# First pair of a two-stage token kernel: GpSimd's own order, b2 as a split row on TensorE, low parts last in group 0

## What is computed

```
h   = relu(x @ W1[lang] + b1[lang])                 # 512 -> 128
y   = x + h @ W2[lang] + b2[lang]                   # 128 -> 512
x1  = x + (y - mean(y)) * rsqrt(var(y) + 1e-5) * gamma[lang] + beta[lang]
g   = gelu(x1 @ M1 + c1)                            # 512 -> 2048
out = x1 + concat(g @ M2 + c2, g @ E[expert] + e[expert])   # 384 and 128 columns
```

## Time and profile before

| | |
|---|---|
| median of 3 runs | 1502.94 us |
| profiled execution | 1501.87 us |
| its span | 1499.8 us |
| TensorE matmul busy | 1460.2 us, 97% |
| VectorE, ScalarE, GpSimd busy | 941.4, 519.4, 648.9 us |
| granted TensorE clock, mean | 0.99 |

### The profile page before, as it was taken

One profiled execution on the slowest core, in us unless ns is written; L12 is line 12 of the kernel. 1 busy time (PEld: TensorE's weight loads), 2 busy tenths in 40 slices (PEclk: granted clock), 3 DMA queues, 4 the chain that ended last, 5 costly groups with the idle time before them and its releaser, 6 DMA issues.

```text
span 1499.8 us, 19043 instructions
## 1 busy us (share of the span) xinstructions
PE 1460.2 (97%) x6428; PEld 1191.3 (79%) x6428; DVE 941.4 (63%) x1598; ACT 519.4 (35%) x837; POOL 648.9 (43%) x641
## 2 busy tenths in 40 slices
PE   8779899999999999999999999999999999999999
PEld 4567788778888888888888888888888888888887
DVE  4757776667557675567655766657755767554444
ACT  1633334323253333432353322532325333332321
POOL 5492534635148341473335533463514834153111
PEclk9989999999999999999999999999999999999999
DMA  7636546655355644645556453665535663454332
GB/s 259 224 108 222 195 155 238 218 165 190 132 179 209 200 153 144 239 163 176 176 170 237 164 171 130 228 218 165 190 126 177 216 200 124 150 173 163 119 139 89
DMA packets 127760, 265.90 MB, mean 177 GB/s; under 512 B 11696, under 2 KB 83632, under 8 KB 119472
## 3 DMA queue, kind: packets, MB, share of 16 engines
q1 hardware_dynamic: 117296, 157.73, 33.0%
q10 hardware_dynamic: 10368, 106.96, 18.9%
HBM read 226.90 MB, written 37.75 MB: 176 GB/s over the span
## 4 chain that ended last, share of the span: by engine, by line
PE 81%; POOL 7%; DMA 3%; DVE 3%; issue 2%; ACT 1%; SPq 1%; POOLq 0%; DVEq 0%; ACTq 0%
PE down L220 14%; PE down L222 14%; PE down L221 14%; PE up_b L220 5%; PE up_b L221 5%; PE up_b L222 5%; PE up_c L220 3%; PE up_a L222 3%; PE up_a L221 3%; PE up_a L220 3%; PE up_c L221 3%; PE up_c L222 3%; POOL resid L855 3%; DMA w_raw<-m_we 2%; DMA w_raw<-m_w 1%
## 5 line engine op out<-in xcount | busy, mean ns | idle before, releaser
L220 PE MATMUL down<-w,g 128*128 128x512 f32 x1024 | 402.8, 393 | 3.4 <-issue 2.8
L221 PE MATMUL down<-w,g 128*128 128x512 f32 x1024 | 399.9, 391 | 0.0
L222 PE MATMUL down<-w,g 128*128 128x512 f32 x1024 | 399.9, 390 | 0.0
L862 POOL TENSOR_TENSOR w<-w_raw,ones 128x256 fp32r<-128x256 f32 x128 | 90.4, 706 | 628.8 <-DMA w_raw<-m_we 628.8
L621 DVE TENSOR_TENSOR g<-g_raw,g 128x512 fp32r<-128x512 f32 x256 | 203.5, 807 | 225.4 <-ACT g L468 225.4
L220 PEld LDWEIGHTS down<-w,g 128*128 128x128 f32 x1024 | 193.4, 189 | 44.8 <-issue 3.2
L222 PEld LDWEIGHTS down<-w,g 128*128 128x128 f32 x1024 | 193.2, 189 | 40.7
L221 PEld LDWEIGHTS down<-w,g 128*128 128x128 f32 x1024 | 193.4, 189 | 39.5
L466 ACT ACTIVATE g_raw<-up_a,m_b_sb 128x512 f32<-128x512 f32 x64 | 44.2, 690 | 372.0 <-PE up_a L222 371.9
L468 ACT CAST g<-g_raw 128x512 fp32r<-128x512 f32 x256 | 159.1, 621 | 8.1
L220 PE MATMUL up_b<-bo,w 128*128 128x512 f32 x384 | 149.7, 390 | 1.4 <-DVE bo L707 1.2
(11 more groups left out here) (165 smaller groups left out, 2360.7 us busy)
## 6 DMA issues: line engine op xcount, KB each, us to landing
w<-w_kept ACTq DMA_DIRECT2D x56, 1792.0 KB, 7.9
w<-w_kept SPq DMA_DIRECT2D x56, 768.0 KB, 5.3
w_raw<-m_we SPq DMA_DIRECT2D x128, 128.0 KB, 4.8
out<-resid SPq DMA_DIRECT2D x64, 256.0 KB, 4.8
xTs_raw<-xT SPq DMA_DIRECT2D x56, 256.0 KB, 3.0
w_kept<-w SPq DMA_DIRECT2D x8, 1792.0 KB, 7.5
xs<-x SPq DMA_DIRECT2D x56, 256.0 KB, 4.8
aw_raw<-a_w SPq DMA_DIRECT2D x30, 256.0 KB, 5.2
```

Of the source, the lines that this page charges most:

```text
L220: eng.matmul(bank, a_hi, b_hi, start=opens, stop=False, skip_group_check=True)
L221: eng.matmul(bank, a_hi, b_lo, start=False, stop=False, skip_group_check=True)
L222: return eng.matmul(bank, a_lo, b_hi, start=False, stop=closes, skip_group_check=True)
L862: eng.tensor_tensor(hi, values, ones[:, :, :].to_broadcast([P, 2, PART]), ALU.mult).then_inc(pool_eh[b], 1)
```

## The change

The order of the first pair on GpSimd, VectorE and ScalarE is written anew, and the opening is changed; all later pairs keep their order.

- GpSimd, opening: x + b2 is gone. x + beta, the roots and the sums of group 0 (in two parts) are interleaved by hand.
- GpSimd, groups: `pool_first_step` replaces `pool_step`. Residual sums of batch 0 go to group 0, those of batch 1 to the end of group 2; roots come first in a group; expert weights go ahead of the weight sums.
- b2 of the first pair is loaded as one row (2 KB), split by ScalarE and VectorE, and added on TensorE for both batches by two one-row passes in fp32r.
- ScalarE, opening: its first activation is Gelu, not Relu; loads of x for batch 0 come behind it; loads of batch 1 behind the split of b2; w1's and w2's high parts of group 0 come earlier.
- VectorE: w1's low part of group 0 between the batches; T2 ahead of T3; in group 0 the low parts of B21 ahead of q; w2's low part and those of C12 and C22 of group 0 move into group 1, behind the sum C21.
- SP: w1's raw weights of group 0 are loaded before batch 1's vectors.
- TensorE: 36 warming transposes for 20; p1 of group 0 behind the transposes; in group 0 each product makes its passes with high x parts first and those with low x parts last, with a wait for each part by itself (`new_product`); B21's transposes go to two free banks.
- The first pair's order of T parts is T1, T2, T3, T4.

```diff
-    WARMING = 20
+    WARMING = 36
+    def new_product(eng, i, bank, of_w, of_x, opens, closes):
+        for c in range(2):
+            s = slice(c * P, (c + 1) * P)
+            if of_x in B_ORDER:
+                eng.wait_ge(act_bhi, i.count(6, B_ORDER.index(of_x) * 2 + c + 1))
+            else:
+                eng.wait_ge(act_thi, i.count(8, t_order(i).index((of_x, c)) + 1))
+            x_hi = bo[:, of_x, c, HI, :]
+            eng.matmul(bank[:, :], w1[:, 0, HI, of_w, s], x_hi, start=opens and c == 0, stop=False, skip_group_check=True)
+            eng.matmul(bank[:, :], w1[:, 0, LO, of_w, s], x_hi, start=False, stop=False, skip_group_check=True)
+        for c in range(2):
+            ...
+            last = eng.matmul(bank[:, :], w1[:, 0, HI, of_w, s], bo[:, of_x, c, LO, :], start=False,
+                              stop=closes and c == 1, skip_group_check=True)
...
     def pe_first_tile(eng, b, t, bank):
+        eng.wait_ge(in_x[b][t], 16)
...
+        eng.matmul(bank[:, :], ident[:, :], xs_tile(first, b, t), start=True, stop=False, skip_group_check=True)
+        if t == 0:
+            eng.wait_ge(act_ones, 1)
+            eng.wait_ge(dve_b2lo, b + 1)
+        row = b2_row(b)[0]
+        eng.matmul(bank[:, :], ones_row[0:1, :], row[:, HI, :], start=False, stop=False, skip_group_check=True)
+        eng.matmul(bank[:, :], ones_row[0:1, :], row[:, LO, :], start=False, stop=False, skip_group_check=True)
...
+    def pool_first_step(eng, i, m, k):
+        if k == 0:
+            pool_aw_lo(eng, m, 0, 0)
+            pool_t_lo(eng, i, T4, 0)
+            pool_t_lo(eng, i, T4, 1)
+            for t in range(TT):
+                pool_residual(eng, i, 0, t)
+        pool_roots(eng, m, k)
+        if k == 4:
+            pool_biases(eng, m, 1, 0)
+            pool_biases(eng, m, 1, 1)
+        if k % 2 == 1:
+            pool_expert(eng, i, 0, k - 1)
+            pool_expert(eng, i, 1, k - 1)
+        elif k > 0:
+            pool_expert(eng, i, 1, k - 1)
+        if k == 1:
+            pool_aw_lo(eng, m, 0, 1)
+            pool_expert(eng, i, 0, 1)
+        if k == 5:
+            pool_biases(eng, m, 1, 2)
+            pool_biases(eng, m, 1, 3)
+        if 1 <= k < GROUPS - 1:
+            pool_weight_sums(eng, k + 1)
+        if k == 2:
+            pool_aw_lo(eng, m, 1, 0)
+        ...
+        if k in (1, 2):
+            pool_biases(eng, m, 0, 2 * k - 2)
+            pool_biases(eng, m, 0, 2 * k - 1)
+        if k == 2:
+            for t in range(TT):
+                pool_residual(eng, i, 1, t)
...
         @block.scalar
+            for k in range(KC):
+                load_xT(eng, first, 0, k)
             eng.wait_ge(pool_c, 4)
-            eng.activation(act_spare[:, :], minus_half[:, :], ACT.Relu).then_inc(act_ready, 1)
+            eng.activation(act_spare[:, :], minus_half[:, :], ACT.Gelu).then_inc(act_ready, 1)
+            eng.copy(ones_row[:, :], ones_row_raw[:, :]).then_inc(act_ones, 1)
+            load_x(eng, first, 0)
+            act_b2_hi(eng, 0)
+            for k in range(KC):
+                load_xT(eng, first, 1, k)
+            load_x(eng, first, 1)
             act_relu(eng, first, 0)
+            act_b2_hi(eng, 1)
+            act_w1_hi(eng, 0)
             act_relu(eng, first, 1, up_a)
...
         @block.vector
+            dve_b2_lo(eng, 0)
             for t in range(TT):
...
             dve_first_finish(eng, 0, 3, FIRST_BANKS[0][3])
+            dve_w1_lo(eng, 0)
             for t in range(TT):
...
             dve_first_finish(eng, 1, 3, FIRST_BANKS[1][3])
+            dve_b_lo(eng, first, B11, 0, down[1])
+            dve_b_lo(eng, first, B11, 1, down[2])
...
         @block.gpsimd
-            for t in range(TT):
-                pool_first_x_b2(eng, t)
-            for t in range(TT):
-                pool_first_x_beta(eng, 0, t)
-                pool_rsqrt(eng, first, 0, t)
-            pool_weight_sums(eng, 0)
```

More of the change, by code:

```diff
@@ L236, in pe_p1 @@
             eng.wait_ge(in_w1[k % 2], i.count(8 * GROUPS, 16 * (k // 2 + 1) - 8 * GROUPS))
[L237 to L240, removed]
+        if k == 0 and i is not first:
+            eng.wait_ge(act_b12, i.count(2, 2))
         if i is not first or k > 0:
@@ L245, in pe_p1 @@
             eng.wait_ge(dve_u, m.front(2 * TT, b * TT + t + 1))
[L246 removed]
+        up_product(eng, i, up_a, k, A11, B11, True, False).then_inc(pe_p[1], 1)
     def pe_p5(eng, i, m, k):
[L249 to L250 removed]
+        if k == 0 and i is not first:
             eng.wait_ge(dve_blo, i.count(6, 3))
@@ L354, in pe_first_tile @@
         s = slice(t * P, (t + 1) * P)
[L355 to L367, removed]
+        eng.wait_ge(in_x[b][t], 16)
+        if b == 1 and t > 0:
+            eng.wait_ge(dve_x1, 1 if t == 1 else TT)
+        eng.matmul(bank[:, :], ident[:, :], xs_tile(first, b, t), start=True, stop=False, skip_group_check=True)
[5 more added lines that the diff above has]
+        eng.matmul(bank[:, :], ones_row[0:1, :], row[:, LO, :], start=False, stop=False, skip_group_check=True)
         if t == 0:
@@ L382, in pe_step @@
         pe_p5(eng, i, m, k)
-        if k == 0:
-            if i is not first:
-                eng.wait_ge(dve_c21, i.count(GROUPS, 0))
+        if k == 0 and i is first:
+            pe_transpose(eng, i, 0, 2, down[1])
+            pe_transpose(eng, i, 0, 3, down[2])
+        elif k == 0:
+            eng.wait_ge(dve_c21, i.count(GROUPS, 0))
             pe_transpose(eng, i, 0, 2, up_b)
@@ L552, in act_step @@
         if k == 0:
-            act_b21_hi(eng, i, 0, up_b)
-            act_b21_hi(eng, i, 1)
+            act_b21_hi(eng, i, 0, down[1] if i is first else up_b)
+            act_b21_hi(eng, i, 1, down[2] if i is first else aux)
             act_t_hi(eng, i, T4, 0)
@@ L741, in dve_step @@
             dve_sum_c21(eng, i, k - 1)
+            if i is first and k == 1:
+                dve_w2_lo(eng, 0)
+                dve_g_lo(eng, i, 0, C12)
+                dve_g_lo(eng, i, 0, C22)
         elif i is not first:
@@ L749, in dve_step @@
             dve_g_lo(eng, before(i), GROUPS - 1, C21)
+        if i is first and k == 0:
+            dve_b_lo(eng, i, B21, 0, down[1])
+            dve_b_lo(eng, i, B21, 1, down[2])
         dve_sum_q(eng, i, k)
+        if i is first and k == 0:
+            dve_t4(eng, i, 0, down[1])
+            dve_t4(eng, i, 1, down[2])
         if i is first and k % 2 == 1:
             dve_w2_lo(eng, 1 if k == 1 else k - 1)
-        if k == 0:
+        if k == 0 and i is not first:
             dve_t4(eng, i, 0, up_b)
@@ L808, in dve_step @@
             dve_b_lo(eng, m, B22, 0, up_c)
-        dve_g_lo(eng, i, k, C12)
-        dve_g_lo(eng, i, k, C22)
         if i is first and k % 2 == 1 and k > 1:
             dve_w2_lo(eng, k)
+        if i is not first or k > 0:
+            dve_g_lo(eng, i, k, C12)
+            dve_g_lo(eng, i, k, C22)
     def pool_aw_lo(eng, m, b, n):
```

208 lines of the change are left out of this document (121 added, 87 removed).

## The result

| | before | after |
|---|---|---|
| median (lowest to highest) | 1503.54 us (1499.26 to 1504.81), 4 runs | 1477.09 us (1476.38 to 1479.82), 4 runs |
| profiled execution, span | 1501.87, 1499.8 us | 1477.28, 1475.5 us |
| first product of group 1 | 65.63 us | 61.48 us |
| first product of the second pair | 240.71 us | 221.85 us |

The ratio of after to before is 0.9832, with a 95% interval of 0.9809 to 0.9856: 26 us faster by the medians, 24.6 between the profiled executions. The forecast was 1474, 27.9 less than the profiled execution. The total is 3 us off; two larger errors of opposite sign stand behind it.

A forecast was written before the change was run, and what follows sets the result against it. TensorE, busy in 97% of the span, bounds the kernel; the first pair's long waits stand behind GpSimd's order. Gains 2.3 + 3.6 + 22 = 27.9 off the profiled 1501.87 give 1474 us, range 1466 to 1488.

The forecast's parts named there:

- its signs: First pair: group 1 starts near 60, no later TensorE wait over 1.5 us, idling about 12 in 200 us, roots ready.
- The opening: Start up to the last finished tile: last finish at 40.7 instead of 43.0, gain 2.3 us, bounds -6 and +5.
- From there to group 1: Last finish to group 1's first product: 19 us instead of 22.6, gain 3.6, product at 59.7.
- T4's 2.5 to 3.0: GpSimd in group 0, before group 1: T4's two low parts were to take 2.5 to 3.0 us.
- GpSimd's chain: GpSimd's work from the last finish to group 1's first product, put at 17 us.
- Part 1: GpSimd's new order in groups 0 to 7 of the first pair: gain 22 us.
- (b): Adapter product at 107.98: residual sums no longer ahead of the adapter's low part; wait 5.73 and slow stretch removed, 7.8.
- (c) and (d): Sum u: roots ahead of weight sums on GpSimd remove waits of 7.6 and 1.6 of slow clock, sum 9.2.
- (a): Group 1's down product: experts split ahead of the weights' wait remove 2.8 of idling and 2.9 of slow clock, 5.7.
- the tie: Group 2's start: weights ready 17.2 after group 1's first product, TensorE ready after 17.1; 0.7 taken off.
- rival 1: GpSimd too slow for its new list, sums of groups 2 and 3 come 3 us later: 6 lost, 1480; chance 0.17.
- rival 4: Clock stays at half level from 38 us on through short waits; to 110 us it is 1508; chance 0.03.

The follow-up runs named there:

- edit 8: The changed kernel with 20 warming transposes instead of 36: 1482.97 us, ratio 0.9895.
- edit 9: The changed kernel with 20 warming transposes instead of 36, run a second time for one execution: 1481.83 us.
- the second profile: The kernel before, unchanged, profiled once more in one execution: 1503.87 us.
- Edit 6: The changed kernel; in group 0 T4's low parts go ahead of the adapter's, p4 ahead of the adapter product, C22 ahead of xT's low parts: 1476.68 us.
- the order alone: The kernel before with only GpSimd's new order in the groups of the first pair, without the new opening and passes: 1488.22 us, ratio 0.9914.
- Edit 4: The changed kernel with batch 0's residual sums moved from group 0 to behind group 2's weight sums: 1475.24 us, ratio 0.9806.
- edit 11: The changed kernel with Edit 4 and Edit 6, batch 1's residual sums two biases earlier, and moments late only in group 5: 1471.80 us, ratio 0.9793.
- the shifted kernel: The kernel before with 70 warming transposes instead of 20, one execution: 1501.15 us.

## Why the prediction was right, and where it was wrong

Of its signs, group 1's first product near 60 came (61.48) and the roots were ready. Two did not hold: waits over 1.5 us remain from there on (1.89 at 68.99, 1.95 at 183.39), and TensorE idles 17.4 us in the first 200, not 12.

**The opening (2.3 forecast, 2.2 measured)** was right in its steps. The last finish came at 40.13 + 0.74 = 40.87, forecast 40.7, before 43.06. A tile was forecast at 2.57 us and took 2.57 (12.73 to 15.29): the price of a one-row pass from the float32 form held. The relu was forecast at 13.7; the first W2 product, behind the row passes, began at 14.33 and waited for nothing. The warming ended at 7.73 and the up product took 3.70; that the longer warming bought this is not shown, as edits 8 and 9 have the same 3.70 with 20 transposes. The 2.2 is against the first profile of before; in the second one the last finish came at 44.29, and it would be 3.4.

**From there to group 1 (3.6 forecast, 2.0 measured, 3.8 against the second profile).** Group 1's first product came at 61.48, not at 59.7. The step that failed is "T4's 2.5 to 3.0" of GpSimd's chain: these two low parts took 4.75 beside w1's low part, 2 more than allowed for, and p4 waited 1.93 for them. GpSimd's chain, put at 17, took 20.2 (40.87 to 61.09). Edit 6 gave them their 2.53 back and gained nothing, as the same two engines then met one instruction later.

**Part 1 (22 forecast, 14.7 measured in the first pair; 13.0 to 13.6 with the order alone).** (b), (c) and (d) held: 7.05 against 7.8 in group 2, 2.4 and 7.0 against 2.4 and 5.2 + 1.6 in groups 3 and 5. The term that failed is (a), 5.7 less 0.7 for the tie, of which group 1 showed 1.3. The old wait went, as said. But the sums of group 2 began 14.1 us after group 1's first product (75.53 against 61.48), not 10: residual sums 6.7 instead of 5.5, starting 0.4 us before that product and not 1, and the next seven expert and adapter pieces 7.8 (67.75 to 75.53) instead of 5.5. Group 2's first product waited 1.22. That was rival 1's place and sign. Rival 1 counted GpSimd alone, though. The larger loss ran the other way: residual sums stretched VectorE's low parts of g, q came late, TensorE waited 1.89 and then ran slowly. Group 1 adds up: 72 matmuls at 0.227 are 16.3, waits 1.89 + 1.22 = 3.1, and 48 matmuls from 68.99 in 14.05 - 1.22 = 12.8 instead of 10.9 are 1.9; together 21.3 of 21.56. Edit 4 took the residual sums away from there, and 3.6 of these 5.0 came back.

Here the Trainium skill (SBUF — State Buffer, "SBUF: two separate sides") had been weighed for GpSimd only. It says that either engine can lose the lock; the trace agrees, with 2.84 and 5.18 us for the same three low parts on VectorE. The trace of before showed it already. The prediction set the residual sums at 81.68 beside w1's low part (79.05), but that ended at 81.13; beside them ran two low parts of g, which had taken 1.28 at 66.37 with GpSimd idle:

```profile
81.05 2.90 DVE L621 TENSOR_TENSOR g<-g_raw,g 128x512 fp32r<-128x512 f32 x2
```

**Two small losses that were not forecast:** 1.3 in group 4 and 1.8 in group 6, of which edit 11 settles the second: the sum C21 behind moments on VectorE.

**What was not in the prediction at all** is the 4.9 behind the first pair. I took all behind 225 us as unchanged. The change does not settle it either: in edit 9, which is the changed kernel but for its warming, part of it is back (2.8 us of waits). The rows of before showed 8.0 us of idling behind 200 us, and I did not ask what held it. This gain hid that the first pair gave 18.9 and not 27.9. The fall of the total near the forecast is therefore partly luck: with that wait still there, it would have been 1482. Why the expert's weights land late in before stays open; shown is that they do in both profiles of before and not in the one of the shifted kernel.

The slow clock (rival 4) did not last: 0.66 from 70 to 75 us, 1.00 from 75 to 80. Its price was put too high: half pace from 38 to 110 us is 36 us of work, less 4 counted already 32, so 1506 and not 1508.

## What to carry to other kernels

Filling an idle engine is not free when the engine beside it works on the same memory: before moving 6 us of GpSimd's elementwise work into a gap, look at what VectorE does in that gap, whose queue TensorE waits on, and price both lists at their shared pace. After removing the longest waits, compare by group with the engine's own work (matmuls times their pace): what is over shows the next wait, however small. And when the start of a program moves by microseconds, waits for transfers much later may come or go; a change of some 5 us in a part that was not edited is to be tested by shifting the unchanged kernel, in more than one execution.

## What the runs showed of the hardware

- VectorE and GpSimd, both on float32 operands in SBUF, slow each other: on GpSimd a 128x512 low part takes 1.27 us alone and 2.4 beside a low part of w1, a residual sum 1.48 to 2.1; on VectorE two low parts of g take 1.28 alone and 2.90 beside residual sums, three take 2.84 or 5.18, w1's of 128x1792 2.01 to 3.10.
- A wait of 1.89 us at 68.99 was followed by matmuls 0.43 us apart from 70.53 to 73.95, near the 1.2 GHz level (mean granted clock from 70 to 75 us 0.66). One of 1.22 at 83.04 was not: the clock of the 24 us behind it was 1.00, the 2.4 GHz level. The first up product, behind 20 transposes, took 5.40 after 2.21 us of idling (before) and 3.70 after 1.59 (edit 8).
- A one-row fp32r pass of 512 columns costs 0.33 us from start to start (13.68 to 14.01) beside the 0.227 of a full one.
- 36 transposes of 128x128 took 5.99 us where 20 took 4.53: the last 16 cost 0.09 each.
- One kernel's opening can differ by 3.1 us between two executions: group 1's first product came at 65.63 and 68.73.
